# A gated FFN layer re-laid as (image, token, unit group), and padding columns dropped from the convolution's buffers

## The reference, cut to what matters

```
def act_quant(x):
    scale = 127.0 / jnp.clip(jnp.max(jnp.abs(x), axis=-1, keepdims=True), 1e-05)
    return jnp.clip(jnp.round(x * scale), -128, 127) / scale
...
def _L1_ffn_ref(x, w1, conv_w, conv_b, w2):
    h = bit_linear(x, w1)                                   # 256 -> 1024 units
    h = depthwise_conv1d(h.transpose(0, 2, 1), conv_w, conv_b)   # 3 taps along the tokens
    h = h.transpose(0, 2, 1)
    h = jax.nn.silu(h)
    return bit_linear(h, w2)                                # 1024 -> 256
...
h = h + _L1_ffn_ref(_layernorm(h, axis=-1), ...)
```

## Time and profile before

| what | us |
|---|---|
| median of 3 runs | 924.82 (922.55 to 928.59) |
| the profiled execution: its own time | 923.76 |
| the profiled execution: its span, first to last instruction | 921.9 |
| DVE busy in the span | 600.6 |
| ACT busy in the span | 439.0 |

### The profile page before, as it was taken

How to read it: one execution, slowest core, us unless ns; L and a number is a source line. 1 busy time by engine, 2 the same in 40 slices (tenths; PEclk the granted TensorE clock), 3 DMA queues, 4 the chain that set the end, 5 groups by cost and what they waited for, 6 DMA issues and landing times.

```text
span 921.9 us, 20693 instructions
## 1 busy us (share of the span) xinstructions
PE 795.2 (86%) x7145; PEld 697.2 (76%) x7145; DVE 600.6 (65%) x1444; ACT 439.0 (48%) x1048; POOL 382.2 (41%) x514
## 2 busy tenths in 40 slices
PE   2899999999999999249999299999999999999633
PEld 2788888998898888126676289898888888888532
DVE  0256665666666654452222035889999999999893
ACT  0244444344444442212222156767778777876552
POOL 0224444444444432222221376646665666543100
PEclk9999999999999996569999699989999999999755
DMA  5316630100000022112212100000000000000000
GB/s 159 90 53 208 184 85 17 19 11 8 8 8 10 11 78 75 41 27 67 70 54 57 28 10 14 8 7 14 19 15 14 15 14 15 18 10 8 9 11 12
DMA packets 23981, 36.41 MB, mean 39 GB/s; under 512 B 10037, under 2 KB 21210, under 8 KB 23114
## 3 DMA queue, kind: packets, MB, share of 16 engines
q1 hardware_dynamic: 14474, 26.20, 10.1%
q0 software_dynamic: 5808, 5.63, 2.8%
q10 hardware_dynamic: 3600, 3.28, 1.1%
HBM read 27.21 MB, written 7.88 MB: 38 GB/s over the span
## 4 chain that ended last, share of the span: by engine, by line
PE 42%; DVE 31%; issue 13%; DMA 7%; ACT 4%; POOL 2%; SPq 1%; DVEq 0%; ACTq 0%; POOLq 0%
PE bank_h L1431 4%; PE bank_c L1468 4%; DMA h<-in_txt 4%; PE bank_b L1459 3%; PE bank_e L1586 3%; PE bank_c L1602 2%; DVE stats L899 2%; PE bank_f L1586 2%; PE bank_d L1602 2%; DVE diff L1107 2%; DVE w L1164 2%; PE bank_b L1500 2%; DVE w L1133 2%; DVE rowmax L1099 2%; DVE w L1139 2%
## 5 line engine op out<-in xcount | busy, mean ns | idle before, releaser
L454 POOL TENSOR_TENSOR qbd<-qt,consts_f 128x560 f32<-128x560 f32 x128 | 163.1, 1280 | 199.5 <-PE bank_e L1403 75.7
L462 POOL TENSOR_TENSOR veps<-mv,consts_f 69x2 f32<-69x2 f32 x64 | 12.4, 194 | 148.7 <-DVE mv L903 110.8
L581 ACT ACTIVATE pt<-bank_g 69x448 f32<-69x448 f32 x64 | 34.9, 546 | 76.6 <-PE bank_h L1413 76.6
L1468 PE MATMUL bank_c<-patches,w_tok 128*128 128x74 f32 x384 | 52.4, 292 | 13.8 <-DMA br<-in_br 13.8
L576 ACT ACTIVATE prob<-diff 112x345 f32<-112x345 f32 x64 | 31.4, 491 | 65.5 <-DVE diff L893 65.5
L1468 PEld LDWEIGHTS bank_c<-patches,w_tok 128*128 128x128 f32 x384 | 50.2, 209 | 13.8 <-issue 13.8
L732 ACT ACTIVATE w<-w,conv 128x138 f32<-128x138 f32 x128 | 54.8, 492 | 10.4 <-DVE w L1116 10.4
L500 POOL DMA_INDIRECT diff<-expert_rows,tile_tokens x25 | 25.5, 1018 | 80.1 <-PE bank_a L1578 59.0
L1777 PE MATMUL bank_b<-f,w 128*69 128x256 bf16 x256 | 37.4, 309 | 15.4 <-ACT w L745 14.5
L481 POOL DMA_INDIRECT expert_lists<-token_no,slot_i x32 | 38.5, 1203 | 21.6 <-issue 14.3
L1431 PE MATMUL bank_h<-values,pt 69*69 69x68 f32 x512 | 39.4, 233 | 8.7 <-ACT pt L581 6.8
(11 more groups left out here) (237 smaller groups left out, 2349.3 us busy)
## 6 DMA issues: line engine op xcount, KB each, us to landing
w<-in_w SPq DMA_DIRECT2D x2, 4096.0 KB, 16.0
patches<-in_patches SPq DMA_DIRECT2D x16, 222.0 KB, 2.6
expert_results<-prob ACTq DMA_DIRECT2D x25, 128.0 KB, 1.9
expert_rows<-x SPq DMA_DIRECT2D x16, 138.0 KB
out<-h SPq DMA_DIRECT2D x16, 138.0 KB
f_raw<-in_f SPq DMA_DIRECT2D x2, 1024.0 KB, 8.1
patches<-in_b SPq DMA_DIRECT2D x1, 2048.0 KB, 10.3
wqkv<-in_wqkv SPq DMA_DIRECT2D x2, 768.0 KB
```

The source lines that it names most:

```text
L454: pool.tensor_tensor(qbd[u % 2][:], q.broadcast_to([128, NG, HPB, QG]), head_mask.unsqueeze(1).unsqueeze(3).broadcast_to([128, NG, HPB, QG ...
L1468: ins = mm(banks["c"][:, m * 2 * IMG:(m + 1) * 2 * IMG], w_tok[:, c, m * 128:(m + 1) * 128], patch_v[:, bass.ds(s, 1), c, :].rearrange("p ...
```

## The change

`hs`, `yc` and the two tap buffers lose the 70th place of each row of tokens: they are now (j, b, t) with 69 tokens side by side. `z` is laid out as (b, t, j), but every stage still addresses it through a view that calls its dimensions (j, b, t), so no stage's instruction count or shape in elements changes. In memory, two neighbours in j are now 4 bytes apart, and two neighbours in t, which was the innermost step of every stage but `hidden_max`, are 8 elements (32 bytes) apart. `hidden_max` therefore reads z in unit step. `gate_hidden`, whose views go as (j, b t), reads and writes z in steps of 32 bytes; so does `scale_gated` and so does `round_up`; `tanh` writes z, and `round_down` reads it, in such steps. `zb` and its 70 places stay.

```
-        cut = lambda i: ffn[:, i * NW:(i + 1) * NW].rearrange("p (j b t) -> p j b t", j=HFC, b=2)
-        hs, yc, z = cut(0), cut(1), cut(2)
+        NT = HFC * 2 * T
+        cut = lambda i: ffn[:, i * NW:i * NW + NT].rearrange("p (j b t) -> p j b t", j=HFC, b=2)
+        hs, yc = cut(0), cut(1)
+        z = ffn[:, 2 * NW:2 * NW + NT].rearrange("p (b t j) -> p j b t", j=HFC, b=2)
...
             def gate_hidden(p):
 
                 dve.wait_ge(F["tanh_made"], p + 1)
-                rows = lambda v: v[:, :, :, 0:T].rearrange("p j b t -> p (j b) t")
+                rows = lambda v: v.rearrange("p j b t -> p j (b t)")
                 dve.scalar_tensor_tensor(rows(z), rows(z), 1.0, rows(yc), ALU.add, ALU.mult).then_inc(F["z_made"], 1)
```

## The result

The changed kernel takes 998.6 us (median of six runs, 993.7 to 1008.8) against 925.2 for the kernel before: 1.079 times as long, with a 95% interval of 1.073 to 1.086. The forecast was 940, in a range from 912 to 956. The direction was right and the size wrong by a factor of almost five: +73 us where +15 was forecast.

A forecast was written before the change was run, and what follows sets the result against it. DVE was taken to bound the twelve full steps and an engine-to-engine chain the last four. 12 x 0.86 = 10.3 us plus 5.3 at the end, +15.6, gave 940 us, in a range from 912 to 956.

The forecast's parts named there:

- What bounds the kernel: Layer 1: DVE bounds twelve full steps (s = 6 to 17, 21.1 us each); an engine-to-engine chain paces the last four.
- the end: Last four steps, s = 18 to 21: longer `scale_gated`, `round_up` and `round_down` on the path, 0.76 + 3 x 1.52 = 5.3 us.
- `hidden_max` in unit step: DVE's reduction over z: 2059 ns becomes about 1296, minus 0.76 us of DVE a step.
- The price of 32-byte steps on DVE: `gate_hidden` and `scale_gated` on z: 0.76 us more each, to about 2.05; DVE's net +0.76 us a step.
- The row of 64 bytes: Profile row of a DVE reduction reading in 64-byte steps, 0.66 ns an element more, taken as nearest to 32 bytes.
- ACT: the term that was mis-sized: ACT's stages on z: 0.76 us more each for `round_up` and `round_down`, nothing for `tanh`.
- The stand before the gate: DVE waits 0.1 us for ACT's `tanh` before `gate_hidden` in a full step, so the period grows by 0.86 us.
- the prediction's own chain: From the start of `scale_gated` through `round_up`, `round_down` and `tanh`: `tanh` ends at 7.92 us, DVE is due at 7.85.
- The rival that writes cost beside the reads: Strided writes cost too: `tanh` 1.88 us, period about 1.6 us longer, +25.3 us, 949 us; chance 0.20.
- PE's granted clock still 1.00 there: Full steps of the changed kernel, near 21.95 us: PE keeps its full clock, its busy time falling only to 20.4 in 22.
- `project` behind `round_up`: `round_up` delays `move_ot` and PE's `project` by 0.84 us, against a period 0.86 longer: no further cost in full steps.
- Padding: Token rows 276 bytes apart instead of 280: taken as zero, with 1 us in all either way in the range only.

The follow-up runs named there:

- the table of steps: A kernel without the computation, timing one DVE and one ACT instruction at steps of 1 to 35 elements: DVE 0.69 us at step 1, 1.07 at 8; ACT 0.63, 1.12.
- The filled kernel: The changed kernel with 14 bf16 matmuls put on PE ahead of `spread_scale1`'s wait for bank d: 975.2 us, 1.056 times the kernel before.
- the first try at the maximum: The kernel before, with ACT writing |z| contiguously and DVE halving it three times instead of the `hidden_max` reduction: 947.0 us, 1.029 times.

## Why the prediction was wrong, by its own steps

*What bounds the kernel: right.* The twelve full steps carried 60.8 of the 75.3 us, the end 9.5 (forecast 5.3). 5.0 came before s = 6, where at most 0.76 was allowed, and s = 6, counted among the twelve, grew by 1.0 only; it had lasted 26.0 us, with DVE busy 21.5 of them and a granted clock of 0.81. Behind, `tanh` and the gate, which the forecast laid beside `ffn_out`, came onto the path.

*`hidden_max` in unit step: right.* 1288 ns for 1296.

*The price of 32-byte steps on DVE: right kind, a little small.* Gate and `scale_gated` 2.18 us each for 2.05. The row of 64 bytes was near: in the table of steps 64 bytes cost DVE 1.02 us where 32 cost 1.07.

*ACT: the term that was mis-sized.* "I take 0.76 for `round_up` and `round_down`, which read z, and nothing for `tanh`, which only writes it." Measured: 1.10, 1.09 and 1.08. Writes are paid like reads. In unit step ACT is quicker per element than DVE, and in large steps about as slow, so its surcharge is the larger; taking DVE's was too little. The rows show ACT quicker in unit step, 1216 ns against DVE's 1292 for the same elements, but nothing of ACT in large steps. The stand before the gate became 1.7 us, not 0.1. In the trace `round_up` starts 2.22 us after `scale_gated`, `round_down` 2.64 later and `tanh` 2.65 after that, at 7.51; it ends at 9.70, and the gate begins at 9.73. With the measured durations the prediction's own chain gives 9.8 for that end. The way of reckoning held: the full steps at 24.1, 22.7 and 21.6 us are its sums within 0.3 us. The rival that writes cost beside the reads was the true case, and even it, with these sizes, came to +25 (its 12 x 1.6 is 19.2 and not 19.4, which changes nothing).

*"PE's granted clock still 1.00 there": the other step that failed, and a term put at nothing.* I judged it by PE's busy time in a longer step, with no row to show that this decides it, and missed that PE would stand 2.6 us in one wait before `spread_scale1`, since PE runs ahead until it needs the bank that a late DVE frees. The lower clock cost 3.3 us a step in eight of twelve steps. The filled kernel returned some 21 us of the 73. No rival of mine had the clock in it.

*`project` behind `round_up`: priced at nothing, and it stood.* PE waited 1.2 us a step for `move_ot`. It has no price of its own in a step that DVE bounds, but it is part of the idle time.

*Padding: nothing, as said* (925.4 us).

Together: the full steps at the surcharge and the stand, about 35 us; the low clock, 26; the end and the start, 14.5. What stays open is why the clock holds in some full steps and not in others with the same 2.55 us wait (s = 7 to 9 of the changed kernel, and four in the midst of the run with z alone re-laid). The length of the wait alone does not decide it: with 1.4 us in each full step the clock stayed at 1.00, and in the first try at the maximum it fell with no wait above 1.0.

## What to carry to other kernels

A layout that makes one instruction contiguous moves the large step into all the others that touch the tensor, and writes count as reads do: list each instruction with its step in bytes after the change, and look for a layout in which none exceeds 8 bytes or jumps without taking two float32 from the place it jumps to. Price a stage engine by engine; one engine's surcharge is not another's. And where a stand is forecast anywhere, ask where PE will then wait: here a wait of 2.6 us came with 3.3 us more in the step wherever the clock fell, and meaningless matmuls in that place paid for themselves. Where the clock did not fall, they cost 0.46 us a step. Whether the same idle time in smaller pieces would have spared the clock was not tried.

## What was not expected of the hardware

A step of 16 bytes is as dear as one of 140 (DVE 1.06 and 1.09 us for 512 elements, 0.69 in unit step), one of 12 bytes costs 0.84, and one of 8 bytes 0.69, as in unit step. ACT pays 0.49 us for 512 elements where DVE pays 0.38. A reduction over pairs that lie side by side but 1104 bytes from one another runs at the contiguous rate (1288 ns for 1104 elements). The kernel with 14 more matmuls in each step was 2.1% faster than without them. In another kernel here PE's clock fell after waits of PE of about 1.0 us at most.
